# Bias by a VectorE add from a table instead of a TensorE product, in the expert stage of a cross-attention and mixture-of-experts kernel

## What is computed

```python
gate_logits = jnp.einsum('nsd,de->nse', x, gate_w) + gate_b
_, top_idx = jax.lax.top_k(gate_logits, K)                   # K = 2
all_out = jax.nn.relu(jnp.einsum('nsd,edo->nseo', x, expert_w) + expert_b)
sel = jnp.take_along_axis(all_out, top_idx[..., None], axis=2)
return sel.mean(axis=2)                                      # on layernorm(x), added to x
```

## Time and profile before

| | |
|---|---|
| median of 3 runs | 395.16 us (394.85 to 395.56) |
| profiled execution, first to last instruction (span) | 391.2 us |
| TensorE busy | 354.0 us, 90% of the span |
| VectorE busy | 288.3 us, 74% |
| ScalarE busy | 264.0 us, 67% |
| GpSimd busy | 234.1 us, 60% |
| mean granted TensorE clock | 0.984 |

### The profile page before, as it was taken

How to read it: one execution, slowest core, us unless ns; L and a number is a source line. 1 busy time by engine, 2 the same in 40 slices (tenths; PEclk the granted TensorE clock), 3 DMA queues, 4 the chain that set the end, 5 groups by cost and what they waited for, 6 DMA issues and landing times.

```text
span 391.2 us, 10358 instructions
## 1 busy us (share of the span) xinstructions
PE 354.0 (90%) x2507; PEld 289.2 (74%) x2507; DVE 288.3 (74%) x1395; ACT 264.0 (67%) x907; POOL 234.1 (60%) x326
## 2 busy tenths in 40 slices
PE   1989999998999999999999999999998788999940
PEld 0856877786688878888878888788886577888730
DVE  2367887788888889888788888888889566444455
ACT  1347777788878878778888788788787544445430
POOL 4616555468976777677677676776764355455500
PEclk9999999999999999999999999999999999999985
DMA  8964040000000000000000000000000354543178
GB/s 277 349 215 188 7 105 3 1 3 29 0 30 1 30 20 7 27 0 27 14 14 27 0 27 0 27 27 0 30 2 28 95 161 131 148 132 121 34 239 316
DMA packets 15093, 28.27 MB, mean 72 GB/s; under 512 B 2892, under 2 KB 10719, under 8 KB 14416
## 3 DMA queue, kind: packets, MB, share of 16 engines
q1 hardware_dynamic: 11408, 20.25, 16.1%
q0 software_dynamic: 2960, 6.94, 5.0%
q10 hardware_dynamic: 688, 0.64, 0.6%
HBM read 17.81 MB, written 10.91 MB: 73 GB/s over the span
## 4 chain that ended last, share of the span: by engine, by line
PE 65%; DVE 12%; issue 10%; POOL 7%; DMA 2%; ACT 2%; DVEq 0%; SPq 0%; POOLq 0%; ACTq 0%
PE psum L1133 11%; PE psum L672 8%; PE psum L673 8%; PE psum L674 8%; PE psum L1090 7%; PE psum L1203 6%; PE psum L1117 5%; POOL prob L1361 2%; DVE x_all L1554 2%; POOL q_sb L1347 2%; PE psum L1180 2%; DVE nsc L1622 2%; DMA wcat<-in_w_kvc 2%; PE psum L369 2%; PE psum L1012 1%
## 5 line engine op out<-in xcount | busy, mean ns | idle before, releaser
L1228 ACT ACTIVATE prob<-nsc,nmax 128x128 f32<-128x128 f32 x256 | 100.8, 396 | 36.3 <-DVE nmax L1622 35.5
L1347 POOL TENSOR_TENSOR q_sb<-rope_a,rope_b 128x256 f32<-128x256 f32 x64 | 47.5, 742 | 59.2 <-DVE rope_b L1585 55.1
L1361 POOL TENSOR_TENSOR prob<-prob,prec 128x512 f32<-128x512 f32 x64 | 67.2, 1050 | 7.4 <-DVE prec L1593 7.4
L1133 PE MATMUL psum<-kT_all,qT 128*128 (+1 forms) x512 | 68.6, 277 | 1.1 <-ACT qT L1271 1.1
L1622 DVE CUSTOM_DVE_ANT_0 nsc<-psum,mask 128x128 f32<-128x128 f32 x256 | 58.6, 284 | 13.0 <-PE psum L1133 13.0
L1133 PEld LDWEIGHTS psum<-kT_all,qT 128*128 128x128 f32 x512 | 62.1, 192 | 2.7 <-ACT qT L1271 2.4
L1415 POOL DMA_INDIRECT halves<-jout,jidx x33 | 32.2, 976 | 30.3 <-DVE jidx L1526 13.7
L1228 ACT ACTIVATION_READ_ACCUMULATOR prob<-nsc,nmax 128x1 f32 x256 | 48.4, 189 | 0.0
L1090 PE MATMUL psum<-ident,q_sb 128*128 128x128 f32 x256 | 41.9, 286 | 2.2 <-POOL q_sb L1347 1.8
L1090 PEld LDWEIGHTS psum<-ident,q_sb 128*128 128x128 f32 x256 | 26.8, 140 | 21.7 <-POOL q_sb L1347 13.6
L1203 PE MATMUL psum<-pT,v_cur 128*64 128x256 f32 x256 | 41.8, 405 | 0.0
(11 more groups left out here) (204 smaller groups left out, 878.1 us busy)
## 6 DMA issues: line engine op xcount, KB each, us to landing
wanted<-slots SPq DMA_DIRECT2D x33, 129.0 KB, 2.4
wo_raw<-in_w_o SPq DMA_DIRECT2D x2, 1024.0 KB, 14.9
we_raw<-in_expert_w SPq DMA_DIRECT2D x1, 2048.0 KB, 7.8
half<-halves SPq DMA_DIRECT2D x4, 512.0 KB, 7.1
x_all<-in_x SPq DMA_DIRECT2D x2, 640.0 KB, 17.4
slots<-pad_row SPq DMA_DIRECT2D x8, 129.0 KB, 3.4
we_raw<-in_ctx_near SPq DMA_DIRECT2D x1, 1024.0 KB, 11.2
out<-x_all SPq DMA_DIRECT2D x2, 512.0 KB, 4.6
```

Source lines behind the costliest of these rows:

```text
L1133: mm = pe.matmul(B_S[r][:, h, :], qT[r][:, h, :], batch_keys, start=True, stop=True)
L1228: e = act.activation(prob[r][:, h, :], nsc[r][:, h, :], ACT.Exp, bias=nmax[r][:, h:h + 1], scale=-1.0, accum_out=psum_h[r][:, h:h + 1])
L1347: pool.tensor_tensor(q_sb[1 - r][:, :, KVC:P], rope_a[1 - r][:], rope_b[1 - r][:], ALU.add).then_inc(m["rope_joined"], 1)
L1361: pool.tensor_tensor(p[:], p[:], prec[1 - r][:, :].unsqueeze(2).to_broadcast([P, HG, P]), ALU.mult).then_inc(m["prob_normed"], 1)
```

## The change

The bias is no longer a product. One DMA spreads the whole bias vector over all 128 partitions (`bias_all`, 1 MB in SBUF). For each job VectorE adds the expert's 256 columns of it to the product in PSUM and writes `jout` (`add_bias`), and ScalarE's relu works in place on `jout`. For each dense group VectorE adds 512 columns and writes `eout`, ScalarE's relus work in place on it, and the sum of a group is made after the bias add of the next one (`dense_sum`; at a tile's first group before it). The semaphores `jbias_done` and `dbias_done` stand between VectorE and ScalarE, and free the PSUM banks. VectorE now loads the words of the job table into registers too. The branch for other inputs, which does not run here, is changed in the same way.

```diff
@@ small_halves and late_loads
-            dve.wait_ge(S("ld_eb_wg"), 32)
+            dve.wait_ge(S("ld_wg"), 16)
             dve.tensor_copy(wg_hl[:, :, 0, :], wg[:]).then_inc(S("wg_done"), 1)
-            dve.tensor_copy(eb2[:, 0, :], eb[:]).then_inc(S("eb_step"), 1)
...
-            dve.tensor_tensor(eb2[:, 1, :], eb[:], eb2[:, 0, :].bitcast(F32), ALU.subtract).then_inc(S("eb_step"), 1)
-            dve.wait_ge(S("ones_set"), 3)
-            dve.tensor_copy(ones2[:], ones2_f[:]).then_inc(S("eb_step"), 1)
...
-            sp.wait_ge(S("eb_step"), 3)
-            for r in range(2):
-                sp.wait_ge(S("bias_zero"), 1)
-                sp.dma_start(bias2[r:r + 1, :].bitcast(F32), eb2[:, r, :].bitcast(F32)).then_inc(S("ld_bias"), 16)
+            sp.dma_start(bias_all[:], expert_b.rearrange("e n -> (e n)").partition_broadcast(P)).then_inc(S("ld_bias"), 16)
@@ constants (GpSimd)
-            pool.memset(bias2[:].bitcast(F32), 0.0).then_inc(S("bias_zero"), 1)
@@ product (TensorE)
-                at_least(pe, "jrelu_done", j - 1)
+                at_least(pe, "jbias_done", j - 1)
...
-                pe.matmul(z, ones2[:], bias2[:, cols], start=True, stop=False)
                 for c in range(DC):
                     mm = mm3(pe, z, jx_hi[j % 4][:, c, :], jx_lo[j % 4][:, c, :], we_hi[:, c, cols], we_lo[:, c, cols],
-                             start=False, stop=(c == DC - 1))
+                             start=(c == 0), stop=(c == DC - 1))
@@ dense (TensorE)
-                    pe.wait_ge(m["relu_done"], f - 1)
+                    pe.wait_ge(m["dbias_done"], f - 1)
...
-                pe.matmul(z, ones2[:], bias2[:, cols], start=True, stop=False)
@@ job and dense (ScalarE)
-                act.wait_ge(m["je_done"], j + 1)
-                at_least(act, f"put{j % RING}", 16 * (j // RING))
-                act.activation(jout[j % RING][:], JOB_BANK[j % 2][:, 0:O], ACT.Relu, scale=0.5).then_inc(m["jrelu_done"], 1)
+                act.wait_ge(m["jbias_done"], j + 1)
+                act.activation(jout[j % RING][:], jout[j % RING][:], ACT.Relu, scale=0.5).then_inc(m["jrelu_done"], 1)
...
-                act.wait_ge(m["e_done"], f + 1)
+                act.wait_ge(m["dbias_done"], f + 1)
...
-                at_least(act, "acc_step", sum_steps(n - 1, kc + 1 if kc else GPT + 1))
...
-                    a = act.activation(eout[kc][:, e, :], DENSE_BANK[f % 2][:, O * e:O * e + O], ACT.Relu,
+                    a = act.activation(eout[kc][:, e, :], eout[kc][:, e, :], ACT.Relu,
@@ job, add_bias, dense (VectorE)
                 for ahead in next_rows(j):
                     prepare(ahead)
+                add_bias(j)
                 if j in DENSE_AFTER_JOB:
                     dense(DENSE_AFTER_JOB[j])
...
+            def add_bias(j):
+                if j % PACK == 0 and j // PACK + 2 < WORDS:
+                    word(j // PACK + 2)
+                cols = bass.ds(columns_of(j), O)
+                if j == 0:
+                    dve.wait_ge(S("ld_bias"), 16)
+                dve.wait_ge(m["je_done"], j + 1)
+                at_least(dve, f"put{j % RING}", 16 * (j // RING))
+                dve.tensor_tensor(jout[j % RING][:], JOB_BANK[j % 2][:, 0:O], bias_all[:, cols], ALU.add
+                                  ).then_inc(m["jbias_done"], 1)
+
             def dense(f):
+                kc, n = f % GPT, f // GPT
+                if f > 0 and kc == 0:
+                    dense_sum(f - 1)
+                dve.wait_ge(m["e_done"], f + 1)
+                at_least(dve, "acc_step", sum_steps(n - 1, kc + 1 if kc else GPT + 1))
+                dve.tensor_tensor(eout[kc][:].rearrange("p a n -> p (a n)"), DENSE_BANK[f % 2],
+                                  bias_all[:, 512 * kc:512 * kc + 512], ALU.add).then_inc(m["dbias_done"], 1)
+                if kc > 0:
+                    dense_sum(f - 1)
+                if f == DENSE - 1:
+                    dense_sum(f)
+
+            def dense_sum(f):
```

More of the change, by code:

```diff
@@ L702, in general_sp @@
             late_loads(sp, "ld_ctx")
-            sp.wait_ge(S("ld_bias"), 32)
+            sp.wait_ge(S("ld_bias"), 16)
             sp.wait_ge(m["latent_mm"], B - 1)
@@ L800, in tile @@
                     cols = slice(512 * kc, 512 * kc + 512)
-                    pe.matmul(bank[kc][:, :], ones2[:], bias2[:, cols], start=True, stop=False)
                     for c in range(DC):
                         mm = mm3(pe, bank[kc][:, :], xT_hi[0][:, c, :], xT_lo[0][:, c, :], we_hi[:, c, cols], we_lo[:, c, cols],
-                                 start=False, stop=(c == DC - 1))
+                                 start=(c == 0), stop=(c == DC - 1))
                 mm.then_inc(m["g_e_mm"], 1)
@@ L973, in tile @@
                 dve.tensor_scalar(gates[0][:], gt2[:], 0.5, None, ALU.mult).then_inc(m["g_gates"], 1)
+                dve.wait_ge(m["g_e_mm"], t + 1)
                 for e in range(NE):
+                    dve.tensor_tensor(eout[0][:, 1, :], bank[e // 2][:, O * (e % 2):O * (e % 2) + O],
+                                      bias_all[:, O * e:O * e + O], ALU.add).then_inc(m["g_biased"], 1)
                     dve.wait_ge(m["g_relu"], NE * t + e + 1)
@@ L1018, in product @@
                     pe.wait_ge(m["score_max"], 2 * GROUPS)
-                    pe.wait_ge(S("ld_bias"), 32)
                     pe.wait_ge(m["we_lo_done"], EXPERT_PIECES)
-                at_least(pe, "jrelu_done", j - 1)
+                at_least(pe, "jbias_done", j - 1)
                 cols = bass.ds(columns_of(j), O)
                 z = JOB_BANK[j % 2][:, 0:O]
-                pe.matmul(z, ones2[:], bias2[:, cols], start=True, stop=False)
                 for c in range(DC):
                     mm = mm3(pe, z, jx_hi[j % 4][:, c, :], jx_lo[j % 4][:, c, :], we_hi[:, c, cols], we_lo[:, c, cols],
-                             start=False, stop=(c == DC - 1))
+                             start=(c == 0), stop=(c == DC - 1))
                     if c == 0 and j % PACK == 0 and j // PACK + 2 < WORDS:
@@ L1531, in job, with word, columns_of @@
                     prepare(ahead)
+                add_bias(j)
                 if j in DENSE_AFTER_JOB:
                     dense(DENSE_AFTER_JOB[j])
-            def dense(f):
+            words = {}
+            def word(q):
+                words[q] = dve.value_load(job_words[0:1, q:q + 1], min_val=0, max_val=NE ** PACK * O - 1)
+            def columns_of(j):
+                q = (j + PACK - FIRST_PACK) // PACK
+                last = FIRST_PACK - 1 + PACK * q
+                return (words[q] >> (3 * (last - j))) & (O * (NE - 1))
+            def add_bias(j):
[3 more added lines that the diff above has]
+                if j == 0:
+                    dve.wait_ge(S("ld_bias"), 16)
+                dve.wait_ge(m["je_done"], j + 1)
+                at_least(dve, f"put{j % RING}", 16 * (j // RING))
+                dve.tensor_tensor(jout[j % RING][:], JOB_BANK[j % 2][:, 0:O], bias_all[:, cols], ALU.add
+                                  ).then_inc(m["jbias_done"], 1)
+            def dense(f):
+                kc, n = f % GPT, f // GPT
[10 more added lines that the diff above has]
+            def dense_sum(f):
                 kc, n = f % GPT, f // GPT
@@ L1601, in slot @@
                 if isinstance(i, int) and i == GROUPS:
+                    dve.wait_ge(m["words_done"], 1)
+                    word(0)
+                    word(1)
                     prepare(0)
```

31 lines of the change are left out of this document (10 added, 21 removed).

## The result

| | before | changed | ratio (95% interval) |
|---|---|---|---|
| median of 5 runs, us | 395.56 (394.85 to 396.60) | 412.43 (411.13 to 413.81) | 1.0424 (1.0399 to 1.0450) |
| span of the profiled execution, us | 391.2 | 409.4 | |
| TensorE busy, us | 354.0 | 354.3 | |
| VectorE busy, us | 288.3 | 309.4 | |
| mean granted TensorE clock | 0.984 | 0.964 | |

Slower by 16.9 us, where 11.1 were forecast and 411 was the high end. The two profiled executions are 18.2 us apart: each recorded run is 1.7 to 1.9 us longer than its own span, so the profiled execution of the kernel before was a fast one, by an estimate from this about 393 us. TensorE's busy time did not fall although 45 products are gone.

A forecast was written before the change was run, and what follows sets the result against it. It took the expert stage as near TensorE's own pace, with fixed queue order as second limit. Stretches of +5.8, +5.2 and +0.1 sum to 11.1 us on the median of 395.16: 406.3 us, range 401 to 411.

The forecast's parts named there:

- the high end: Whole kernel: 411 us, if register instructions before each bias are not hidden (3.6 more) and the first stretch is at its upper end.
- jobs 0 to 11: First stretch, among the last tiles of attention: +5.2 us from later relus.
- The loop: Expert stage: bias add, relu, jx_hi, jx_lo wait on each other round VectorE and ScalarE, 1.63 us per job.
- From relu 29 to the last store: Job 29 to the last store of halves: 6.9 us against 6.73 today, +0.1 with rounding.
- The first bias adds 0.45: Start of jobs 0 to 11: the first bias add costs 0.45 us.
- From the row to relu 7: Last tile's row, with bias 5 and 6 queued behind it: 5.4 us against 2.98 today, +2.4.
- The other eight steps: Remaining relu-to-relu steps of jobs 0 to 11: 2.4 us, a little under 8 x 0.33 = 2.6.
- Jobs 11 to 29: Six periods of three jobs with one group, plus group 4's extra and job 14's word load: 37.2 us, +5.8.
- a rival at 4%: TensorE's clock falls to 1.2 GHz in the expert stage, six periods take 14.7 us more: 421 us; chance 4%.
- The loads are 11.1 later: End of the kernel: the loads of halves, not VectorE's adds (8.9 later), decide the end: +11.1 us.
- the low end: Whole kernel: 401.5 us, with first stretch 3.6, no word load, group 4's extra hidden, and VectorE's adds deciding the end.
- The rival that work counts: Expert stage keeps TensorE's pace, removed products are the gain: 388.6 us; decided by a turn below 0.93 us; chance 4%.

The follow-up runs named there:

- e3: Changed kernel with filler products keeping TensorE busy in its idle times, ahead of each job's product and the last row's turn: 410.60 us, ratio 1.0392.
- e8: e6 with VectorE's steps of jobs 5 and 6 ahead of the last row, first two word loads behind preparing jobs 0 and 1: 399.63 us.
- e1: Kernel before with VectorE's sum of a dense group made one job later, bias still on TensorE: 391.86 us, ratio 0.9909.
- e11: The same kernel as e1, measured once more: 391.87 us, ratio 0.9914.
- e12: Changed kernel with GpSimd's load of the bias vector into a small unused tile put back: 411.27 us, ratio 1.0415.
- e2: Changed kernel with ScalarE's jx_hi of job j + 3 ahead of the relu of job j from job 11 on: 403.54 us, ratio 1.0189.
- e6: e2 with the dense bias add and dense relus one job later on VectorE and ScalarE: 402.53 us, ratio 1.0190.
- e5: Changed kernel with GpSimd's fill of a tile put back at its old place and the table's load behind it: 409.53 us (one run).

## Why the prediction was wrong in size

The step that failed is the sum by stretch, in its first term above all: +5.2 for jobs 0 to 11 measured +8.2. The loop was right; its surroundings were priced too low, and the clock was left out of the sum.

**Right.** The direction and the mechanism. The loop was put at 1.63 us and is 1.63; bias add 0.42 (0.41 forecast), dense add 0.69 (0.69); three jobs with one group 5.98 us (5.95). A relu took 0.417 us from SBUF against 0.385 from PSUM before, 0.032 more where 0.035 was forecast. The register instructions of the high end are hidden, since the turn is 1.63 us with them. From relu 29 to the last store it took 6.52 us (6.9 forecast). That the loads decide at the end is right. The later sums cost nothing.

**Wrong.** By the profiled executions the forecast lacks 7.1 us of span (18.2 less 11.1), by the medians 5.8. The 7.1, by the terms of the sum:

- Jobs 0 to 11, +5.2, measured +8.2 (33.5 less 25.4). 7.0 of it is there in e3 too, at full clock. "The first bias adds 0.45": relu 0 came 1.3 later after the reciprocal. The first two word loads, with the register instructions behind them, stand ahead of everything on VectorE, which idles 1.20 us there; my step priced a word for job 14 and forgot the first two. In e8, with them behind the preparation, relu 0 came 0.4 earlier. From the row to relu 7, 5.4 forecast, took 6.0, in e3 too: xT_lo of the row and the wait for product 7 stand in it. The other eight steps gave 2.7 in e3 for 2.4. The remaining 1.1 is the clock. VectorE of the changed kernel, and last its word loads and the register instructions behind them (ns min/median/max):

```profile
309.27 0.18 DVE L1611 RECIPROCAL prec<-psum_h 128x4 f32<-128x4 f32 x1 [0.34 <-ACT prob L1209]
310.64 0.21 DVE L1498 TENSOR_SCALAR is_high<-wanted,job_region 128x1 f32<-128x1 f32 x1 [1.20 <-issue]
...
327.82 0.41 DVE L1719 TENSOR_SCALAR row<-x_all,mv,rstd 128x256 f32<-128x256 f32 x1 [2.88 <-POOL rstd L1346]
...
L1519 DVEq TENSOR_LOAD <-job_words x5: 304/307/318, 309.3 to 347.9; - x5
L1519 DVEq FUSED_REGOPS  x5: 183/190/190, 309.6 to 348.2; - x5
```

- Jobs 11 to 29, +5.8, measured +7.0, 0.8 of it the clock: the turn 368.46 to 375.22 took 6.76 us. The rest is small: 0.2 at job 14's word, 0.1 at group 4, 0.2 in six turns of 0.03.
- The clock had been a rival at 4% that held all or nothing, at 421. It came true in three short stretches, 1.9 us together by e3 (1.1 and 0.8). The error was in the form of the rival: TensorE's long idles (at the row, at group 4) were in my own sum, and none was priced as a cause of slower products behind it. I took the first 20 us, at 1.00 with 11.23 busy, as evidence against it; e1 and e11 show the same idles with and without a fall, so such a row could not exclude it.
- I counted the removed work of the opening and the earlier table load at nothing: 1.6 us came before the expert stage, 0.8 in the opening, where other profiles scatter by more, and 0.7 in five steps inside attention, which is real (the changed kernel and its eight variants have it, the kernel before and its four have not) and unexplained.
- "The loads are 11.1 later", with their time kept: their issue took 2.2 us longer, and the end grew by 1.4. Whether one caused the other is not shown: e1 has an issue of 1.64 us without losing by it, and e12, with the changed kernel's steps, has an end of 26.9 us, so the 1.4 can be scatter.
- Two slips changed nothing. The 4.0 us between span and median are not the start and the end of the program: each recorded run is 1.7 to 1.9 us longer than its span, and the rest is that the profiled execution was fast. And the terms of the low end add up to 5.3, which gives 401.0 and not 401.5.
- The rival that work counts is refuted for the changed kernel by e3. Its condition, a turn below 0.93 us, came true in e2, once the loop was open: 0.92. So TensorE's products are worth something only after the order is repaired (28.1 against 29.0 us), and then the first stretch outweighs it.

## What to carry to other kernels

Before moving work to a half idle engine, follow the queues round: an add of 0.42 us closed a loop over four instructions of two engines, and the kernel is 17 us faster without it. Behind a reordered queue, from job 11 on, the same add costs nothing (28.1 us in e6 against 29.0 in e1); among the last steps of attention no order tried here made it cheap. Look for steps in fixed order that wait for a long producer and put them one round later; here this alone, without moving any work, made the kernel faster by 0.9%.

## What the hardware showed beside

- TensorE's granted clock fell to 0.50 behind idles of 1.09, 1.95 and 2.69 us in the changed kernel and came back after 3.4 to 6.8 us. It stayed at 1.00 behind idles of 1.47 to 1.62 us there and of 2.73 us in e5 and e12, and one kernel (e1 and e11) showed a fall in one profile and none in the other.
- Two word loads into VectorE's registers went with an idle of 1.20 us. One load is 0.31 us on VectorE's queue as on TensorE's, and 0.19 us of register instructions follow it.
- The longest issue of one of eight equal loads took 1.1 to 2.1 us in every profile but that of the kernel before (0.60).
